# Spline attention: a running minimum in VectorE's last pass, the gate in two halves around the tanh addition, and the clips one place up

## What is computed

```python
sim = jnp.einsum('bhnd,bhdm->bhnm', q, k) / math.sqrt(dh)
xs = _safe(sim)                                   # clip to [-6, 6]
coef = (spline_w * spline_scaler[..., None])[0, 0]
kan = base_w[0, 0] * jax.nn.silu(xs) + jnp.einsum('...k,k->...', b_splines(xs), coef)
attn = jax.nn.softmax(kan, axis=-1)
out = jnp.einsum('bhnm,bhmd->bhnd', attn, v)
```

## Time and profile before

| | |
|---|---|
| median of 3 runs | 7482.52 us (7480.34 to 7487.51) |
| span of the profiled execution | 7470.2 us, 12.3 us less than the median |
| busy share of the span | PE 90%, DVE 84%, ACT 78%, POOL 72% |
| the spline attention's clips | first 2063.6 us, last 7413.9 us after the span's start |
| instructions | 142915 |

### The profile page before, as it was taken

One profiled execution on the slowest core, in us unless ns is written; L12 is line 12 of the kernel. 1 busy time (PEld: TensorE's weight loads), 2 busy tenths in 40 slices (PEclk: granted clock), 3 DMA queues, 4 the chain that ended last, 5 costly groups with the idle time before them and its releaser, 6 DMA issues. The chain is left out here.

```text
span 7470.2 us, 142915 instructions
## 1 busy us (share of the span) xinstructions
PE 6708.3 (90%) x41336; PEld 4573.5 (61%) x41336; DVE 6259.6 (84%) x9621; ACT 5790.6 (78%) x9066; POOL 5398.4 (72%) x3374
## 2 busy tenths in 40 slices
PE   6877889999789999999999999999999999999998
PEld 4656547777546666666666666666666666666666
DVE  4333664444389999999999999999999999999998
ACT  5454113233189999999999999999999999999998
POOL 4333000000089999999999999999999999999997
PEclk8888999999889999999999999999999999999998
DMA  2000000000110000000000000000000000000000
GB/s 74 19 22 22 1 1 0 0 1 0 54 17 1 1 1 1 1 1 11 1 1 1 1 1 1 2 28 1 1 1 1 1 2 2 4 4 4 4 4 6
DMA packets 75948, 56.12 MB, mean 8 GB/s; under 512 B 50776, under 2 KB 73464, under 8 KB 75032
## 3 DMA queue, kind: packets, MB, share of 16 engines
q1 hardware_dynamic: 72512, 53.88, 2.6%
q10 hardware_dynamic: 3288, 0.33, 0.0%
HBM read 37.80 MB, written 16.37 MB: 7 GB/s over the span
## 5 line engine op out<-in xcount | busy, mean ns | idle before, releaser
L1532 POOL TENSOR_TENSOR a_s<-a_s,a_v 128x784 f32<-128x784 f32 x1568 | 2912.7, 1858 | 307.2 <-ACT a_s L1743 285.7
L1568 PE MATMUL a_right_sides<-a_s,diag_d 128*128 128x392 f32 x6272 | 2284.3, 507 | 8.3 <-POOL a_s L1532 1.0
L1568 PEld LDWEIGHTS a_right_sides<-a_s,diag_d 128*128 128x128 f32 x6272 | 1132.1, 190 | 1052.0 <-POOL a_s L1532 309.2
L1664 DVE SCALAR_TENSOR_TENSOR a_kan<-a_s,spline_c,a_kan 128x784 f32<-128x784 f32 x1568 | 1622.9, 1035 | 50.4
L1591 PEld LDWEIGHTS a_weighed<-a_V,a_probT 112*128 112x128 f32 x10976 | 1374.3, 193 | 162.2
L1525 POOL TENSOR_TENSOR a_inner<-a_inner,a_x 128x784 f32<-128x784 f32 x784 | 1458.5, 1860 | 0.0
L1591 PE MATMUL a_weighed<-a_V,a_probT 112*128 112x65 f32 x10976 | 1365.1, 270 | 0.0
L1743 ACT ACTIVATE a_s<-a_v 128x784 f32<-128x784 f32 x1568 | 1335.6, 852 | 4.7
L1734 ACT ACTIVATE a_v<-a_a 128x784 f32<-128x784 f32 x1568 | 1336.5, 853 | 0.3
L1580 PE MATMUL a_turned<-ident,a_prob 128*112 128x128 f32 x5488 | 856.4, 278 | 230.7 <-ACT a_probT L1750 229.1
L1635 DVE TENSOR_SCALAR a_x<-a_scores 128x392 f32<-128x392 f32 x1568 | 877.5, 560 | 20.2 <-PE a_scores L1555 20.2
(11 more groups left out here) (194 smaller groups left out, 6094.2 us busy)
## 6 DMA issues: line engine op xcount, KB each, us to landing
rows<-bias_rows_dram SPq DMA_DIRECT2D x112, 91.0 KB
X<-in_x_dram SPq DMA_DIRECT2D x4, 1568.0 KB, 13.8
a_q<-q_dram SPq DMA_DIRECT2D x392, 16.0 KB, 2.0
mask<-in_window_mask_dram SPq DMA_DIRECT2D x56, 98.0 KB
v_dram<-V SPq DMA_DIRECT2D x14, 227.5 KB, 2.3
a_V<-v_dram SPq DMA_DIRECT2D x4, 796.2 KB, 9.2
q_dram<-Q SPq DMA_DIRECT2D x14, 224.0 KB, 1.9
k_dram<-K SPq DMA_DIRECT2D x14, 224.0 KB, 1.9
```

The lines of the kernel that those rows point to most:

```text
L1532: eng.tensor_tensor(s, s, v, ALU.mult).then_inc(cubed, 1)
L1568: mm = eng.matmul(up[:, j, 0:SUB], steps[i][:, :], cubes[g][:, SUB * j:SUB * (j + 1)], start=(i == 0), stop=(i == 1))
L1664: eng.scalar_tensor_tensor(F, banked((s1, s2)[j][g][:, :]), c[:, 3 + j:4 + j], F, ALU.mult, ALU.add).then_inc(left_added, 1)
```

## The change

The last pass now accumulates a negated running minimum: `add_right` writes minus the sum to `prob[r]` and carries the minimum from quarter to quarter through the column `gmin[r][:, g-1:g]`, so the fourth quarter's value is already the negated maximum of the row. `exponent` reads it directly as its bias with scale -1, and `row_max` and `negated_max` are gone. `gate` becomes two instructions, one for each bank, one ahead of `add_tanh` and one behind it. The clips stand one place further up, `invert` and `add_output` are moved to stand between `left(g, 1)` and `add_right`. Only DVE's list is written in another order.

```diff
-        gmax = [sb(f"gmax{r}", [P, 4]) for r in range(2)]
-        rmax = [sb(f"rmax{r}", [P, 1]) for r in range(2)]
-        nmax = [sb(f"nmax{r}", [P, 1]) for r in range(2)]
+        gmin = [sb(f"gmin{r}", [P, 4]) for r in range(2)]
...
                 def right_side(g):
-                        eng.wait_ge(right_gated, n + 1)
+                        eng.wait_ge(right_gated, 2 * n + 2)
...
-                def gate(g):
+                def gate(g, j):
                     def stage(eng, t, r, p):
+                        at = slice(SUB * j, SUB * (j + 1))
                         eng.wait_ge(right_made, 4 * t + g + 5)
                         eng.wait_ge(turned, 7 * t + min(2 * g + 2, 7))
-                        eng.scalar_tensor_tensor(banked(part(r, g)), banked(x[g][:, :]), 0.0, U, ALU.is_gt, ALU.mult).then_inc(right_gated, 1)
+                        eng.scalar_tensor_tensor(part(r, g)[:, at], x[g][:, at], 0.0, up[:, j, 0:SUB], ALU.is_gt, ALU.mult).then_inc(right_gated, 1)
...
                         eng.wait_ge(left_added, 2 * n + 10)
+                        if g == 3:
+                            eng.wait_ge(exp_done, 4 * t + 4)
+                        eng.wait_ge(all_added, n + 1)
                         f = banked(part(r, g))
                         eng.sem_inc(waits_met_v, 1)
-                        eng.tensor_tensor_reduce(out=f, in0=F, in1=f, scale=1.0, scalar=-3.0e38, op0=ALU.add, op1=ALU.max,
-                                                 accum_out=gmax[r][:, g:g + 1]).then_inc(all_added, 1)
+                        eng.tensor_tensor_reduce(out=f, in0=F, in1=f, scale=-1.0, scalar=gmin[r][:, g - 1:g] if g else 3.0e38, op0=ALU.add, op1=ALU.min,
+                                                 accum_out=gmin[r][:, g:g + 1]).then_inc(all_added, 1)
...
-                    (g2, l2), (g3, l3) = (((g - back) % 4, int(g < back)) for back in (2, 3))
-                    between = {1: ([(invert, 3)], []), 2: ([], [(add_output, 4)]), 3: ([(row_max, 1)], [(negated_max, 1)])}.get(g, ([], []))
-                    order += [(add_tanh(g3), l3)] + between[0] + [(times_x(g3), l3)] + between[1] + [(left(g3, 0), l3), (clip(g, 0), 0), (left(g3, 1), l3),
-                              (clip(g, 1), 0), (add_right(g3), l3), (gate(g2), l2)]
+                    g3, l3 = (g - 3) % 4, int(g < 3)
+                    between = {1: [(invert, 3)], 2: [(add_output, 4)]}.get(g, [])
+                    order += [(gate(g3, 0), l3), (add_tanh(g3), l3), (gate(g3, 1), l3), (times_x(g3), l3), (clip(g, 0), 0), (left(g3, 0), l3),
+                              (clip(g, 1), 0), (left(g3, 1), l3)] + between + [(add_right(g3), l3)]
...
                 def exponent(g):
                     def stage(eng, t, r, p):
-                        eng.wait_ge(max_ready, t + 1)
-                        eng.activation(part(r, g), part(r, g), ACT.Exp, bias=nmax[r][:, :]).then_inc(exp_done, 1)
+                        eng.wait_ge(all_added, 4 * t + 5)
+                        eng.activation(part(r, g), part(r, g), ACT.Exp, scale=-1.0, bias=gmin[r][:, 3:4]).then_inc(exp_done, 1)
```

More of the change, by code:

```diff
@@ L1458, in kan_attention3 @@
         (loaded, q_ready, inverted, heads_folded, o_ready, y_made, x_added, out_stored, margin_set, s_made, clipped, v_ready, s_ready, cubed, line_made, inner_made, tanh_made, with_tanh, based, left_added,
-         right_made, right_gated, all_added, max_found, max_ready, exp_done, turned, copied, weighed, placed, waits_met_v, waits_met_p) = (
+         right_made, right_gated, all_added, exp_done, turned, copied, weighed, placed, waits_met_v, waits_met_p) = (
             sem(n) for n in ("loaded", "q_ready", "inverted", "heads_folded", "o_ready", "y_made", "x_added", "out_stored", "margin_set", "s_made", "clipped", "v_ready", "s_ready", "cubed", "line_made", "inner_made",
-                             "tanh_made", "with_tanh", "based", "left_added", "right_made", "right_gated", "all_added", "max_found",
-                             "max_ready", "exp_done", "turned", "copied", "weighed", "placed", "waits_met_v", "waits_met_p"))
+                             "tanh_made", "with_tanh", "based", "left_added", "right_made", "right_gated", "all_added",
+                             "exp_done", "turned", "copied", "weighed", "placed", "waits_met_v", "waits_met_p"))
         with nc.Block() as block:
@@ L1597, in project_out @@
                     eng.wait_ge(x_added, t + 4)
-                    eng.wait_ge(right_gated, 4 * t + 16 if not isinstance(t, int) else min(4 * t + 16, 4 * BLOCKS3 + 1))
+                    eng.wait_ge(right_gated, 8 * t + 32 if not isinstance(t, int) else min(8 * t + 32, 8 * BLOCKS3 + 2))
                     rows = slice(VW * (p % 2), VW * (p % 2 + 1))
@@ L1685, in invert @@
                     eng.reciprocal(rinv[:, :], op[:, VW:V1]).then_inc(inverted, 1)
-                def row_max(eng, t, r, p):
-                    eng.wait_ge(all_added, 4 * t + 5)
-                    eng.tensor_reduce(rmax[r][:, :], gmax[r][:, :], AX.X, ALU.max).then_inc(max_found, 1)
-                def negated_max(eng, t, r, p):
-                    eng.wait_ge(max_found, t + 1)
-                    eng.wait_ge(exp_done, 4 * t + 4)
-                    eng.tensor_scalar(nmax[r][:, :], rmax[r][:, :], -1.0, None, ALU.mult).then_inc(max_ready, 1)
                 dve.sem_inc(clipped, 2)
@@ L1698, in _ @@
                 dve.sem_inc(left_added, 8)
-                dve.sem_inc(right_gated, 1)
+                dve.sem_inc(right_gated, 2)
                 dve.sem_inc(all_added, 1)
```

2 lines of the change are left out of this document (1 added, 1 removed).

## The result

The changed kernel takes **8776.82 us** (median of 4 runs, 8772.53 to 8779.33), the kernel before 7481.43 us (4 runs, 7480.09 to 7487.51). The ratio is 1.173 (95% 1.1714 to 1.1747). The profiled execution has a span of 8770.8 us, against 7470.2. Spread over the 192 steps in which `add_output` meets a `right_side(0)`, that is 1300.6 / 192 = 6.77 us a step, 34.09 instead of 27.32.

The account below looks back on a forecast made before the run. DVE, busy 395.29 of 400 us, was taken to bound the kernel, with ACT, POOL and PE close behind. DVE's own edits cancel; 7482.5 + 879 (two chains) + 422 (clock) = 8784 us, range 8320 to 9180.

Parts of the forecast that it names:

- Who waits for what was moved: Other engines wait for the late invert and add_output; two chains back to DVE add 4.58 us a step, 879 us.
- Chain 1: From invert in slot 1 through ACT's place to slot 2's clip: 5.60 us against DVE's 4.00, costing 1.60 a step.
- Chain 2: From add_output in slot 2 through PE's right_side(0) to slot 3's clip: 6.98 us against 4.00, costing 2.98 a step.
- The clock's term: PE's 3.3 us gap ahead of right_side(0) lowers its clock, slowing the matmuls behind: 2.2 us a step, 422 us.
- The change on DVE alone: In DVE's slot, filled bubbles offset the split gate and a new bubble: 6.82 against 6.83 us, 0 give or take 0.02.
- The clock up (1): Rival: both chains cost time but PE's clock does not fall, 8361 us; chance 0.13.
- PE slow for most of the step (2): Rival: both chains, clock also falls ahead of turn(2), 4 us or more lost a step, 9170 us or more; chance 0.08.
- Only chain 1 (3): Rival: only the late invert costs time, add_output being hidden; 307 us, 7790 us; chance 0.05.
- nothing bites (4): Rival: no engine's wait matters, only DVE's sum; 7482 us, or up to 45 more with the scalar read; chance 0.03.
- the kernel gets faster (6): Rival: last pass starts 0.03 us after left ends, not 0.18; slot 6.67, 118 us less, 7365 us; chance 0.02.
- The order of DVE doesn't matter (5): Rival: DVE's reordering gives and takes nothing, each extra instruction costs; 47 us, 7530 us; chance 0.01.
- The rule on bubbles: On DVE, dependent instructions start 0.13 to 0.28 us later than independent ones, against the skill's rule of an empty pipe.

Follow-up runs that it names:

- Experiment 5: Kernel before with only invert and add_output moved to just ahead of the last pass; gates, clips and row maxima as they were: 8778.86 us, ratio 1.1744.
- experiment 1: Changed kernel with invert alone put back behind add_tanh, add_output left late: 8504.75 us, ratio 1.1376.
- experiment 2: Changed kernel with add_output alone put back behind times_x, invert left late: 8007.02 us, ratio 1.071.
- experiment 3: Changed kernel with invert and add_output both put back, all else as changed: 7683.5 us, ratio 1.0278 to the kernel before.
- experiment 7: Changed kernel with added PE matmuls by zeros, seven ahead of turn(2) and twelve ahead of right_side(0): 8536.18 us, ratio 1.142.
- experiment 8: Kernel before with only the negated running minimum in last pass and exponential, row_max and negated_max gone, old order: 7542.97 us, ratio 1.0099.
- experiment 4: Changed kernel with twelve zero-matrix matmuls added on PE between scores(2) and right_side(0): 9278.43 us, ratio 1.2411.
- experiment 9: Changed kernel reordered: second half gate behind times_x, clips back in old places, invert and add_output behind add_tanh: 7443.44 us, ratio 0.9953 to the kernel before.
- experiment 6: Changed kernel with added PE matmuls using real weights, seven ahead of turn(2) and twelve ahead of right_side(0): 8555.89 us, ratio 1.1446.

## Why the prediction was right, point by point

- **Who waits for what was moved** is shown, not only argued. Experiment 5 gives as large a slowdown from the two moves alone, experiments 1 to 3 give each chain alone, and in the traces of 1 and 5 the wait ahead of `right_side(0)` is put down to `add_output` by name. Chain 1 was forecast at 5.60 us and is 5.62 in the trace. Its price was 1.60 a step; measured are 1.69 between experiments 3 and 2, and 1.42 between the changed kernel and experiment 1. That the chains add holds to within 5%.
- **Chain 2** was forecast at 6.98 without the clock. With the clock held up it is 6.86 (experiment 7). In the changed kernel it is 8.76, of which 1.9 is clock: the right side takes 4.78 instead of 2.90.
- **The clock's term** was right in kind and nearly in size, with its place told too narrowly. Forecast were 2.2 us a step (422 us), all on the matmuls behind the gap of 3.3 us; experiment 7 gives 2.14 (411 us) in all. In the step shown 1.9 of it is where it was forecast. The rest comes from falls around shorter gaps, such as the one of 1.05 ahead of `scores(1)`, which sets a clip back by 0.4 us in that step. That the figure chosen between 0 and 4.25 came so close is partly luck.
- **The change on DVE alone** was mis-sized: "0, give or take 0.02 a slot". Three slots of a step are 6.94 us and the one without a column 6.88 (measured in experiment 3, 5011.84 to 5018.72), together 27.70 against 27.32, some 0.38 a step or 73 us. The prediction took 0 for the column and kept 0.06 as the upper bound; experiment 8 measures 0.06. And the bubble ahead of the last pass is 1.26 in the loop, where the last step's rows gave 1.22. In experiment 2 it is 1.21 or 1.22 in all four slots (such as 5003.84 to 5005.06), so this part depends on something that no run isolates. The split gate cost the 0.06 forecast, and the removed instructions gave nothing, as forecast.
- **The sum.** Without stalls a step is 27.70. In the one shown, chain 1 adds 1.50 over DVE's own 4.12 there and chain 2 adds 4.65 over its own 4.11. Some 0.4 more comes from a clip that waited behind a slow `scores(1)`. That makes 34.25; the mean is 34.09, and the forecast had 27.32 + 4.58 + 2.2 = 34.10. At full clock the forecast had 31.90 and experiment 7 shows 31.95, but two parts of this were off and cancelled. DVE's own work was 0.38 too small. The two chains' excess over it was 0.35 too large: 1.48 and 2.75 a step (5.60 less 4.12, 6.86 less 4.11) instead of 1.60 and 2.98. About two thirds of the second error follow from the first, since DVE's longer work beside a chain is hidden by it; the rest is luck. So 8784 against 8777 us is closer than its parts were. The 12.3 us between span and median are mostly a difference between runs: each run's own time stands 1.7 us above its span (8772.53 and 8770.8).
- **The rivals.** The clock up (1): 8536 to 8556 us is what comes nearest to it, with fillers. Its 8361 was sound for what it assumed: 192 steps of 31.95 would give 8371. PE slow for most of the step (2) did not come, but experiment 4 shows that it can (9278). Only chain 1 (3) is experiment 2: 8007 us, not 7790, because the DVE term and the clock come on top. That nothing bites (4), or that the kernel gets faster (6), fails even without the moves: experiment 3 is 207 us slower than the kernel before. The order of DVE doesn't matter (5) is contradicted by experiment 9: the same passes are 0.5% faster than the kernel before in one order, and 17% slower in the change's.
- **The rule on bubbles** of the Trainium skill (VectorE: DVE Perf Modes, section "The DRAIN you can't avoid"), by which the next op does not start until the pipe is empty, does not fit here: independent passes of 1.03 us start 0.94 apart, dependent ones 1.07 to 1.26. The same section adds that an op that is not held starts earlier, and the 0.94 agrees with that, so the prediction drew on only one half of the section.

## What to carry to other kernels

Before moving a short instruction on the engine that sets the pace, follow who waits for its result, around the loop and back to that engine. Here 0.16 and 0.28 us of work, put some 3 to 4 us later, cost 1093 us in the changed kernel and 1304 in the kernel before, because each stands at the head of a chain that returns to the same engine within a slot or two. Fill bubbles with what nobody waits for (half a gate, a clip), but count each bubble once: what stood in it before costs its own time afterwards (experiment 3). Keep the heads of chains early, and add to every new wait on TensorE the price of a clock that falls while it stands.

## What the runs showed of the hardware beyond that

- **The clock can fall around short gaps, and stay down under load.** Gaps of 0.53, 1.05 and 1.88 us in a PE that was otherwise mostly busy were followed by matmuls at the lower clock (experiments 3 and 4), though not in every step. In the pipeline's filling a gap of 2.11 was not the earlier trace rows. In experiment 4 PE then worked without a pause at about 0.50 from 5008.7 to about 5022 us. The same filler matmuls, begun at full clock, keep it at 0.97 in experiments 6 and 7. The trace doesn't settle why it stayed down for so long. The Trainium skill (TensorE: Matmul & The Clock Gate, section "A second HAM failure mode: psum-queue depth-cycling") tells of a kernel in which frequent short idle spots between groups of matmuls let the clock swing between its two levels; experiment 3 agrees, with scores of 1.58 us instead of 0.89 behind a gap of 1.05.
- **More work made the kernel faster**: 38 extra pieces of matmul a step on the engine that is waited for took 221 to 241 us off. The chains at full clock are as long as forecast without fillers, so it is the clock that gives this back. Here it paid only where the filler starts at full clock (experiment 4 against 6 and 7).
- **A starting value read from an SBUF column** costs the custom pass 0.06 us of 0.97, both in its length (1.03) and in the start of what follows (0.95 against 0.89).
